# One sine product per rotation and NF4 compares from one run of 513 columns to three rows of 171

## The reference

```python
def rope(x, pos):
    ...
    cos, sin = (jnp.cos(emb)[None, None], jnp.sin(emb)[None, None])
    x1, x2 = jnp.split(x, 2, axis=-1)
    rot = jnp.concatenate([-x2, x1], axis=-1)
    return x * cos + rot * sin

def nf4_quant_dequant(w):
    flat = w.reshape(-1, BLOCKSIZE)
    absmax = jnp.max(jnp.abs(flat), axis=1, keepdims=True)
    normalized = flat / jnp.where(absmax == 0, 1.0, absmax)
    bounds = (NF4_CODE[:-1] + NF4_CODE[1:]) * 0.5
    idx = jnp.searchsorted(bounds, normalized)
    return (NF4_CODE[idx] * absmax).reshape(shape)
```

## Time and profile before

| | us |
|---|---|
| median of 3 runs | 1913.04 (1912.93 to 1913.94) |
| the profiled execution, its own time | 1912.8 |
| its span | 1911.0 |
| PE busy | 1834.3 (96%) |
| DVE busy | 1484.2 (78%) |
| ACT busy | 1278.5 (67%) |
| POOL busy | 1264.8 (66%) |

### The profile page before, as it was taken

The page is one execution under the profiler, slowest core; times in us unless marked ns, Lnnn a source line. Parts: engine busy times, 40 slices in busy tenths (PEclk is TensorE's granted clock), DMA queues, the critical chain, the costliest instruction groups (busy, mean ns, idle before and its releaser), DMA issues.

```text
span 1911.0 us, 42834 instructions
## 1 busy us (share of the span) xinstructions
PE 1834.3 (96%) x11439; PEld 1212.8 (63%) x11439; DVE 1484.2 (78%) x3980; ACT 1278.5 (67%) x4967; POOL 1264.8 (66%) x1164
## 2 busy tenths in 40 slices
PE   4899999999999999999999999999989999999997
PEld 3567667676777677667767776776666654444443
DVE  5999899999999888899998889999999956302112
ACT  5688777777777777777777777777677745312121
POOL 2767777777777777777777777777766738212121
PEclk8999999999999999999999999999999999999999
DMA  6101111111111111111111111111211033000000
GB/s 223 54 30 44 38 50 48 46 44 46 45 45 43 43 48 43 43 43 43 43 44 50 43 43 43 43 43 35 85 31 30 24 110 111 34 1 22 0 22 22
DMA packets 85452, 90.51 MB, mean 47 GB/s; under 512 B 14216, under 2 KB 56456, under 8 KB 85384
## 3 DMA queue, kind: packets, MB, share of 16 engines
q1 hardware_dynamic: 85384, 89.71, 15.2%
HBM read 76.48 MB, written 13.18 MB: 47 GB/s over the span
## 4 chain that ended last, share of the span: by engine, by line
PE 49%; DVE 23%; issue 19%; POOL 4%; ACT 2%; DVEq 1%; DMA 0%; POOLq 0%; ACTq 0%
PE bank L1369 12%; PE bank L1398 6%; PE bank L1358 5%; DVE f_s L1061 5%; PE bank L1340 4%; PE bank L1414 4%; PE bank L1496 3%; PE bank L1407 3%; PE bank L1435 3%; DVE f_nrm L1048 2%; PE bank L1324 2%; DVE qtT L961 2%; POOL hl L600 2%; PE bank L1514 2%; DVE qc L909 2%
## 5 line engine op out<-in xcount | busy, mean ns | idle before, releaser
L554 POOL TENSOR_TENSOR f_acc<-f_acc,f_s 128x512 f32<-128x512 f32 x429 | 548.9, 1279 | 32.6 <-POOL f_acc L554 0.4
L1369 PE MATMUL bank<-wh,xh 128*128 (+2 forms) x1024 | 335.0, 327 | 7.5 <-DVE cumh L1210 6.3
L1369 PE MATMUL bank<-wl,xh 128*128 (+2 forms) x1024 | 335.0, 327 | 0.0
L1369 PE MATMUL bank<-wh,xl 128*128 (+2 forms) x1024 | 334.8, 327 | 0.0
L1061 DVE TENSOR_SCALAR f_s<-f_nrm 128x512 f32<-128x512 f32 x480 | 282.1, 647 | 3.5
L538 POOL TENSOR_TENSOR pr<-pr,rp 128x512 f32<-128x512 f32 x128 | 133.3, 1041 | 216.1 <-DVE rp L983 216.1
L651 ACT ACTIVATE qe<-bank,nqm 128x128 f32<-128x128 f32 x512 | 180.9, 365 | 95.7 <-DVE qs L912 84.0
L1496 PE MATMUL bank<-xh,w 128*128 (+3 forms) x704 | 218.4, 379 | 1.7 <-ACT sg L837 1.7
L600 POOL TENSOR_TENSOR hl<-hf,hh 128x512 f16<-128x512 f32 (+1 forms) x44 | 51.3, 1167 | 231.4 <-ACT hh L843 231.4
L1220 DVE SCALAR_TENSOR_TENSOR hf<-bank,sg 128x512 f32<-128x512 f32 (+1 forms) x44 | 30.3, 689 | 221.5 <-PE bank L1496 210.6
L1358 PE MATMUL bank<-wh,oT 128*128 (+1 forms) x512 | 194.0, 379 | 4.4 <-DVE xl L1127 3.6
(11 more groups left out here) (179 smaller groups left out, 4918.9 us busy)
## 6 DMA issues: line engine op xcount, KB each, us to landing
f_blk<-wa SPq DMA_DIRECT2D x33, 320.0 KB, 2.9
f_raw<-wb SPq DMA_DIRECT2D x33, 256.0 KB, 2.7
dequantised<-f_w SPq DMA_DIRECT2D x33, 256.0 KB, 2.0
w<-dequantised SPq DMA_DIRECT2D x33, 256.0 KB, 4.3
raw_qkv<-wq SPq DMA_DIRECT2D x29, 256.0 KB, 2.4
raw_o<-wo SPq DMA_DIRECT2D x29, 256.0 KB, 2.6
f_recb<-scales SPq DMA_DIRECT2D x99, 64.0 KB, 2.6
f_absb<-scales SPq DMA_DIRECT2D x99, 64.0 KB, 2.6
```

The costliest lines, as they stand in the source:

```text
L554: nc.gpsimd.tensor_tensor(f_acc[:], f_acc[:], f_s[:, step, :], ALU.add).then_inc(s["f_ad"], 1)
L1369: last = nc.tensor.matmul(dst, av, w[:, sl + c, lo:hi], start=(n == 0), stop=(n == 3 * NC - 1))
```

## The change

The sine products of both halves become one operation: it reads the two halves of each head in backward order (a step of minus one over the halves) and writes the output straight through. The NF4 buffers get a new shape: `f_nrm` and `f_acc` have 513 columns (the last one is zero), and each of the eight buffers of `f_s` has three rows of 171 columns at a pitch of 172. A compare reads 513 columns in one run and writes three rows. POOL's adds read the three rows and write one run of 513. `cum`, a constant, moves into the space of `f_s`, and one clearing of `f_nrm` is added at the start.

```diff
+NF4_ROWS = 3
+NF4_ROW = 171
-        f_s = sb("f_s", [P, 8, NF4_PIECE])
+        f_s = sb("f_s", [P, 8, NF4_ROWS, NF4_ROW + 1])
-        f_nrm = sb("f_nrm", [P, NF4_PIECE])
-        f_acc = sb("f_acc", [P, NF4_PIECE])
+        f_nrm = sb("f_nrm", [P, NF4_ROWS * NF4_ROW])
+        f_acc = sb("f_acc", [P, NF4_ROWS * NF4_ROW])
+        in_rows = lambda a: a.rearrange("p (a n) -> p a n", n=NF4_ROW)
+        step_rows = lambda k: f_s[:, k, :, 0:NF4_ROW]
...
-                    nc.gpsimd.tensor_tensor(f_acc[:], f_acc[:], f_s[:, step, :], ALU.add).then_inc(s["f_ad"], 1)
+                    nc.gpsimd.tensor_tensor(in_rows(f_acc[:]), in_rows(f_acc[:]), step_rows(step), ALU.add).then_inc(s["f_ad"], 1)
...
+            nc.vector.memset(f_nrm[:], 0.0)
...
-            sin_b = lambda t, half, n: sin[:, t.i % 2, t.p, half, :].unsqueeze(1).to_broadcast([P, n, P // 2])
+            sin_b = lambda t, n: sin[:, t.i % 2, t.p, :, :].unsqueeze(1).to_broadcast([P, n, 2, P // 2])
...
-                nc.vector.tensor_tensor(d4[:, :, 0, :], s4[:, :, 1, :], sin_b(t, 0, n), ALU.mult)
-                nc.vector.tensor_tensor(d4[:, :, 1, :], s4[:, :, 0, :], sin_b(t, 1, n), ALU.mult).then_inc(done, 1)
+                nc.vector.tensor_tensor(d4, s4[:, :, ::-1, :], sin_b(t, n), ALU.mult).then_inc(done, 1)
...
-                    nc.vector.tensor_scalar(f_s[:, k % 8, :], f_nrm[:], float(BOUND[k]), float(DELTA[k]),
+                    nc.vector.tensor_scalar(step_rows(k % 8), in_rows(f_nrm[:]), float(BOUND[k]), float(DELTA[k]),
                                             ALU.is_gt, ALU.mult).then_inc(s["f_sd"], 1)
...
-                nc.vector.scalar_tensor_tensor(out=f_dq[:], in0=f_acc[:], scalar=float(CODE[0]), in1=f_absb[:],
+                nc.vector.scalar_tensor_tensor(out=f_dq[:], in0=f_acc[:, 0:NF4_PIECE], scalar=float(CODE[0]), in1=f_absb[:],
                                                op0=ALU.add, op1=ALU.mult).then_inc(s["f_dqd"], 1)
```

More of the change, by code:

```diff
@@ L196, in layer @@
         cau = sb("cau", [P, 512], BF16)
-        cum = sb("cum", [P, 130])
         cumh = sb("cumh", [P, 130], F16)
@@ L224, in layer @@
         su = SM[:, 0:P]
-        stage = f_s[:].rearrange("p a n -> p (a n)")
+        in_rows = lambda a: a.rearrange("p (a n) -> p a n", n=NF4_ROW)
+        step_rows = lambda k: f_s[:, k, :, 0:NF4_ROW]
+        stage = f_s[:].rearrange("p a b n -> p (a b n)")
+        cum = stage[:, 3840:3970]
         w_raw = [raw_qkv[:]] + [stage[:, 1536 + 768 * j:2304 + 768 * j] for j in range(NC - 1)]
@@ L237, in layer @@
         w12_at = [at["raw_qkv"], at["wl"], at["wl"] + 4096, at["qrT"], at["wh"] + 10240, at["wh"] + 14336, at["wl"] + 10240,
-                  at["wl"] + 14336, at["f_s"] + 8192, at["f_s"] + 12288, at["qc"]]
+                  at["wl"] + 14336, at["f_s"] + 8256, at["f_s"] + 12352, at["qc"]]
         w3_at = [at["pa"], at["pa"] + 2048, at["oT"], at["va"], at["vm"], at["qtT"], at["qtT"] + 2048, at["pr"],
@@ L423, in _ @@
             for dst, src in ((cos[:], cosc), (sin[:], sinc), (stage[:, 0:1024], winmask), (stage[:, 1024:1536], causal),
-                             (cum[:], cumsum), (keep[:], keepc)):
+                             (cum, cumsum), (keep[:], keepc)):
                 sp.dma_start(dst, src).then_inc(s["consts"], 16)
@@ L550, in add_step @@
                         pool.wait_ge(s["f_dqd"], j)
-                    nc.gpsimd.tensor_tensor(f_acc[:], f_s[:, first, :], f_s[:, step, :], ALU.add).then_inc(s["f_ad"], 1)
+                    nc.gpsimd.tensor_tensor(in_rows(f_acc[:]), step_rows(first), step_rows(step), ALU.add).then_inc(s["f_ad"], 1)
                 elif k > 1:
                     pool.wait_ge(s["f_ad"], j * 14 + (k - 1))
-                    nc.gpsimd.tensor_tensor(f_acc[:], f_acc[:], f_s[:, step, :], ALU.add).then_inc(s["f_ad"], 1)
+                    nc.gpsimd.tensor_tensor(in_rows(f_acc[:]), in_rows(f_acc[:]), step_rows(step), ALU.add).then_inc(s["f_ad"], 1)
             def nf4_add(t):
@@ L1047, in nf4_scaled @@
                 dve.wait_ge(s["f_rec_in"], j * 80 + 80)
-                nc.vector.tensor_tensor(f_nrm[:], f_raw[:], f_recb[:], ALU.mult).then_inc(s["f_nrmd"], 1)
+                nc.vector.tensor_tensor(f_nrm[:, 0:NF4_PIECE], f_raw[:], f_recb[:], ALU.mult).then_inc(s["f_nrmd"], 1)
                 dve.wait_ge(s["f_nrmd"], j + 1)
@@ L1067, in late_nf4 @@
                         dve.wait_ge(s["f_ad"], 14 * STEPS + max(k - 4, 1))
-                    nc.vector.tensor_scalar(f_s[:, k % 4, :], f_nrm[:], float(BOUND[k]), float(DELTA[k]),
+                    nc.vector.tensor_scalar(step_rows(k % 4), in_rows(f_nrm[:]), float(BOUND[k]), float(DELTA[k]),
                                             ALU.is_gt, ALU.mult).then_inc(s["f_sd"], 1)
@@ L1209, in _ @@
             nc.vector.tensor_copy(cau[:], stage[:, 1024:1536]).then_inc(s["z_id"], 1)
-            nc.vector.tensor_copy(cumh[:], cum[:]).then_inc(s["z_id"], 1)
+            nc.vector.tensor_copy(cumh[:], cum).then_inc(s["z_id"], 1)
             dve.wait_ge(s["z_id"], 7)
```

## The result

| | before | after |
|---|---|---|
| median of 4 runs each, us | 1912.99 (1912.75 to 1913.94) | 1899.99 (1898.27 to 1901.45) |
| the profiled execution, us | 1912.8 | 1898.27 |

The account below looks back on a forecast made before the run. PE bounds the kernel, busy 96%, losing 1.10 us a step to others, mainly late VectorE work. 1912.8 - 3.4 (loop) - 5 (first steps) - 6.5 (last steps) = 1897.9, median 0.24 higher: 1898 us; range 1880 to 1911, 8 in 10.

Parts of the forecast that it names:

- The compares' new price: Each compare on VectorE, writing three rows on one port, takes 0.60 us start to start, without waiting for POOL.
- The rival that keeps both ports: Compares still use both ports, so only the sines count: 1908 us; chance 0.12.
- Turn D: Loop: four compares 2.48 us against 3.66, sine -0.06, so PE's wait for `qtT` goes: -0.40 us a step.
- Turn A: Loop, ahead of `kt`: two compares +0.52, sine of k -0.06, `f_nrm` -0.20; together +0.26 us a step.
- Turns B and C: Loop: slower compares, about +1.0 and +0.42 us, hidden by 0.6 and 0.3 us to spare before PE asks for `qtT`.
- the rival without margins: Spare time of turns B and C is not there; 0.2 and 0.3 us lost: +12, 1910 us; chance 0.12.
- The sines: One sine product instead of two on VectorE saves 0.06 us each for q and k, 0.12 a turn.
- the slower rival: Backward order of the sine product runs at half rate, adding 0.66 us a turn: 1938 us; chance 0.08.
- The ends: Written-out steps ahead of and behind the loop: PE waits less for `kt` and `qtT`, -5 and -6.5 us.
- The loop's forecast: Sum of the turns in the loop: net -0.14 us a step, 24 steps, -3.4 us.
- POOL's adds read three rows ... I take 0: POOL's adds cost nothing more for reading rows: 0; bounds nothing below, 0.1 us an add above.
- a gain for `f_nrm`: Turn A: `f_nrm` starts earlier since POOL no longer waits 0.78 us for `rp` in turn D; 0.2 us left.

Follow-up runs that it names:

- the run of 513: Changed kernel with the compares' 513 output columns written as one run of 513 instead of three rows; 1907.35 us.
- `f_safe` free: `f_safe` made by one maximum with a tiny constant, one SBUF input, three rows of five; on the changed kernel 1895.64 us.
- the best kernel: Changed kernel with turn A's two compares on two ports, `f_safe` free, and `f_dq` moved behind the merge of `pr` in turn B; 1883.80 us.

## Why the prediction was right, and where it was not

The time was forecast at 1898 and measured at 1899.99, the direction at 0.73. Taken by its steps:

- **The compares' new price**, taken as 0.60 from start to start, is that (2.46 us for four), in every turn, and 296.0 us in all against the 288 I gave; the difference is in recorded lengths, which overlap. The rival that keeps both ports is refuted by the durations, and the run of 513 shows what it would have given: 1907.35, against 1908 worked out.
- **Turn D**: forecast -0.40, measured -0.42, and PE's wait there is gone.
- **Turn A**: forecast +0.26, measured +0.21. Of its terms, the two compares' 0.52 was measured as 0.53 by the run with two ports in turn A. The sine alone took 0.05 off (forecast 0.06). `f_nrm` is 0.18 shorter (forecast 0.2), for the reason given: POOL doesn't wait for `rp` in turn D and so starts `qc` as early as `qs` lets it. The kernel with the accumulator in rows and `f_safe` free has slow adds and the same `f_nrm` (1.38), so this doesn't hang on the adds.
- **Turns B and C** kept their cover: no new wait in either, as forecast; the rival without margins falls.
- **The sines**: one operation of 0.682 for q and 0.283 for k, no slower backward than forward, so the slower rival falls too. The sine alone gave 5.9 us (6.9 against the kernel before that ran beside it), where 3 and about 2 were worked out.
- **The ends** gave 3.8 and 5.3 instead of 5 and 6.5, the loop 5.1 instead of 3.4. In the first steps the waits for `kt` grew from 4.0 to 6.3 us, where I allowed "about 1". The compares are some 1.3 of it: with `f_safe` free the same waits come to 5.3 us. Free of it, the ends give 6.1 and 6.6 us (199.9 and 227.9 against 206.0 and 234.45), near the forecast. The loop's forecast of -0.14 a step came from differences of small terms; -0.22 was measured.

**The step that failed** is "POOL's adds read three rows ... I take 0". I looked at `pr`, which reads four rows, found no cost and stopped; I bounded only a loss. The adds became 0.12 us shorter each, 56 us of POOL's time. Worse, my price of 0 was not harmless even so. At exactly that price, with adds of 1.28 us, the kernel takes 1925.65: slower than before. The reason is an operation that the prediction never named, `f_safe`, ten columns wide, which then comes just behind the start of an add in every step of the loop and waits it out, ahead of all that leads to `kt`. The prediction even had the cause in hand, POOL 0.2 us and more earlier in turn A, and booked it only as a gain for `f_nrm`. The chances gave such a mechanism no case of its own. With this meeting out of the way the same slow adds give 1901.35, 3 us from the forecast: the sum was right for a kernel in which `f_safe` is never held up. That it was right for this one too is owed to the faster adds, which in the loop let `f_safe` slip in behind the last of them. In this respect the prediction was lucky.

And the mechanism it told, compares that leave POOL's port, is only one way to this gain. Four rows of 128 keep both ports, speed the adds up as well, and reach the same time (1900.77), or 9.7 us less than the one-port form once `f_safe` is free.

What stays open: why an add is faster when its two inputs have different patterns. The runs show that it is so in two shapes and undone in two, not what in POOL does it. And the 0.44 us a step that the best kernel still loses.

## What to carry to other kernels

When an access pattern changes, read again how long the operations take on every engine that uses the buffer, as well as on the one that the change is meant for. Before counting on "it doesn't wait for POOL", list all DVE operations that can, those of ten columns too, with their place in POOL's row: one of 0.17 us that falls into an add of 1.27 us took up to 1.19, and here 0.24 us decided whether it did. One port is a choice for each operation: with five compares in turn D it kept that turn at its floor where two ports left it at 12.11, and it was wrong where POOL rests and the operation stands ahead of what PE waits for (15.2 us here for two compares a step). How much it is worth depends on POOL's adds: once they are fast and `f_safe` is free, all compares on two ports (1885.95) come within 2.2 us of the best kernel.

## What was new about the hardware

- A POOL addition of two f32 inputs of 512 or 513 columns took 1.27 us when both were runs (513 columns too, 1.274), 1.28 when both were rows, and 1.15 (3 x 171) or 1.18 (4 x 128) when one was a run and the other in rows. The first add of a piece, of two inputs in rows, kept its 1.28 in the kernel in which the other 429 became faster.
- A DVE product that reads halves of 64 columns of PSUM in backward order took 0.682 us for 512 columns, the same as the forward product beside it (0.681).
- A DVE operation of ten columns with both inputs in SBUF took 0.17 us or up to 1.19, by where it fell in POOL's row of adds; the wait is inside its recorded duration, so no view of waits shows it. `em` (line 1010 of the changed kernel), one column wide, took 0.87 us beside POOL's first add, and 0.15 in the kernel with five compares a turn, where that add isn't there.
